# One reduction instruction for the scores of two heads in the maximum pass

## What is computed

```python
scores = jnp.einsum('bhqd,bhkd->bhqk', q, k) / jnp.sqrt(jnp.float32(dk))
scores = jnp.where(mask[:, None, None, :] == 0, neg_inf, scores)
scores = jnp.where(future[None, None, :, :], neg_inf, scores)
attn = jax.nn.softmax(scores, axis=-1)
context = jnp.einsum('bhqk,bhkd->bhqd', attn, v)
```

## Time and profile before

| | |
|---|---|
| median of 3 runs | 720.61 us (720.42 to 721.02) |
| span of the profiled execution | 718.9 us |
| TensorE busy | 653.6 us, 91% |
| VectorE busy | 516.2 us, 72% |
| ScalarE busy | 386.0 us, 54% |
| maximum pass on VectorE (L892) | 640 reductions, 333.1 us |

### The profile page before, as it was taken

One profiled execution on the slowest core, in us unless ns is written; L12 is line 12 of the kernel. 1 busy time (PEld: TensorE's weight loads), 2 busy tenths in 40 slices (PEclk: granted clock), 3 DMA queues, 4 the chain that ended last, 5 costly groups with the idle time before them and its releaser, 6 DMA issues.

```text
span 718.9 us, 11481 instructions
## 1 busy us (share of the span) xinstructions
PE 653.6 (91%) x4148; PEld 346.1 (48%) x4148; DVE 516.2 (72%) x1071; ACT 386.0 (54%) x762; POOL 68.8 (10%) x122
## 2 busy tenths in 40 slices
PE   5424989999989999999899999899998999999996
PEld 2313545546544345444333343333321388888885
DVE  4113888776897987787889788888944288777764
ACT  2210246664766675665867756567788633432331
POOL 3030440140001000220000000000000000000000
PEclk9775999999999999999999999899999999999999
DMA  9599697018001000039200130000000430607000
GB/s 297 90 136 131 109 127 78 3 36 98 2 2 19 2 1 1 2 74 160 77 1 1 45 74 1 1 1 2 1 2 1 67 52 1 133 17 140 6 31 30
DMA packets 36464, 36.87 MB, mean 51 GB/s; under 512 B 4471, under 2 KB 31447, under 8 KB 36408
## 3 DMA queue, kind: packets, MB, share of 16 engines
q1 hardware_dynamic: 33878, 33.65, 27.4%
q10 hardware_dynamic: 2530, 2.50, 1.1%
HBM read 27.94 MB, written 7.77 MB: 50 GB/s over the span
## 4 chain that ended last, share of the span: by engine, by line
PE 78%; DMA 9%; DVE 6%; ACT 3%; issue 2%; SPq 1%; POOL 1%; DVEq 0%; ACTq 0%; POOLq 0%
PE bank L1158 17%; PE ring L1118 15%; PE bank L1142 15%; PE ring L1219 4%; DMA qaug<-q_parts 4%; PE ring L1220 4%; PE ring L1221 4%; PE ring L1050 4%; PE bank L1050 4%; DVE pmax L892 3%; DMA q_parts<-stage 2%; PE bank L1236 2%; PE bank L1238 2%; PE bank L1237 2%; DMA k_parts<-stage 2%
## 5 line engine op out<-in xcount | busy, mean ns | idle before, releaser
L892 DVE TENSOR_REDUCE pmax<-ring 128x1 f32<-128x512 f32 (+4 forms) x640 | 333.1, 576 | 86.5 <-PE ring L1121 43.9
L769 ACT ACTIVATE probs<-bank 128x512 f32<-128x512 f32 (+4 forms) x592 | 286.7, 550 | 133.4 <-PE bank L1142 84.7
L1118 PE MATMUL ring<-kaug,qaug 97*128 97x512 bf16 (+4 forms) x640 | 201.9, 345 | 29.1 <-DMA qaug<-q_parts 23.3
L1142 PE MATMUL bank<-qaug,kaug 99*128 99x512 bf16 (+4 forms) x592 | 201.9, 357 | 6.4 <-ACT probs L769 5.5
L1158 PE MATMUL bank<-probs,vaug 128*32 128x512 f32 (+4 forms) x1184 | 143.2, 556 | 0.0
L1118 PEld LDWEIGHTS ring<-kaug,qaug 97*128 97x128 bf16 x640 | 61.3, 99 | 158.3 <-DVE pmax L892 82.2
L1142 PEld LDWEIGHTS bank<-qaug,kaug 99*128 99x128 bf16 (+1 forms) x592 | 57.2, 99 | 66.8 <-ACT probs L769 32.4
L796 ACT ACTIVATE u_sb<-u_sb 128x512 f32<-128x512 f32 x32 | 20.2, 632 | 59.2 <-DVE u_sb L1005 59.1
L1219 PE MATMUL ring<-x_hi,w_hi 128*128 128x512 f32 x128 | 50.4, 394 | 0.0
L1220 PE MATMUL ring<-x_lo,w_hi 128*128 128x512 f32 x128 | 50.2, 392 | 0.0
L1221 PE MATMUL ring<-x_hi,w_lo 128*128 128x512 f32 x128 | 49.8, 389 | 0.0
(11 more groups left out here) (110 smaller groups left out, 641.7 us busy)
## 6 DMA issues: line engine op xcount, KB each, us to landing
qaug<-s_dram SPq DMA_DIRECT2D x4, 2048.0 KB, 15.5
qaug<-q_parts SPq DMA_DIRECT2D x24, 256.0 KB, 9.3
kaug<-k_parts SPq DMA_DIRECT2D x18, 256.0 KB, 9.3
q_parts<-stage SPq DMA_DIRECT2D x8, 384.0 KB, 2.6
k_parts<-stage SPq DMA_DIRECT2D x6, 384.0 KB, 12.0
x_sb<-in_x ACTq DMA_DIRECT2D x4, 512.0 KB, 11.8
w_sb<-in_w SPq DMA_DIRECT2D x4, 512.0 KB, 5.4
out<-x_sb SPq DMA_DIRECT2D x4, 512.0 KB, 3.2
```

Source lines behind the costliest of these rows:

```text
L769: act.activation(probs[0:rows, u % NSLOT, h, off:CH], side_bank(e)[0:rows, off:CH], ACT.Exp, scale=DK ** -0.5).then_inc(side_read, 1)
L892: dve.tensor_reduce(pmax[:, n % 2, qt, h, slot:slot + 1], bank[:, 0:w], AX_X, ALU.max).then_inc(ring_read, 1)
L1118: last = pe.matmul(bank[:, b0:b1], qaug[0:ROW_MAX, c % 2, 4 * g + h, P * qt:P * (qt + 1)], kaug[0:ROW_MAX, 4 * g + h, k0 + b0:k0 + b1], st ...
L1142: last = pe.matmul(bank[0:r, off:CH], kaug[0:ROWS, 4 * g + h, P * j:P * j + r], qaug[0:ROWS, c % 2, 4 * g + h, off:CH], start=True, stop=n ...
```

## The change

Two heads of a group form one item. `max_pieces` yields (query tile, pair of heads, first key, width, diagonal, slot), the pair outermost; there are half as many items. Every `mx` item takes two ring banks and starts on an even one. TensorE writes the first head's scores into the first bank and the second head's into the second, each with its mask where it is on the diagonal, and signals once, after the last. VectorE reduces both with one instruction over a view of 128 partitions, 2 banks, w columns, into two neighbouring heads of `pmax`. `max_schedule` counts such an item for twice its width, so that the pace in columns is as before. Nothing else is changed.

```diff
+GP = 2
@@ max_pieces
-    for h in range(4):
+    for pr in range(GP):
...
-                out.append((qt, h, k0, w, i < KT and k0 + w == seen, slot))
+                out.append((qt, pr, k0, w, i < KT and k0 + w == seen, slot))
@@ max_schedule
-        total = sum(w / P for _, _, _, w, _, _ in pieces)
+        total = sum(2 * w / P for _, _, _, w, _, _ in pieces)
...
-            done += w / P
+            done += 2 * w / P
@@ ring_places
-        banks = 2 if e[0] == "mx" and max_pieces(e[1])[e[2]][3] > CH else 1
+        banks = 2 if e[0] == "mx" else 1
@@ ring_bank
-            return ring[:, CH * first:CH * (first + (2 if e[0] == "mx" and first % 2 == 0 else 1))]
+            return ring[:, CH * first:CH * (first + (2 if e[0] == "mx" else 1))]
@@ VectorE, mx
-                    qt, h, k0, w, _, slot = max_pieces(n)[k]
-                    dve.tensor_reduce(pmax[:, n % 2, qt, h, slot:slot + 1], bank[:, 0:w], AX_X,
+                    qt, pr, k0, w, _, slot = max_pieces(n)[k]
+                    dve.tensor_reduce(pmax[:, n % 2, qt, GP * pr:GP * (pr + 1), slot],
+                                      bank.rearrange("p (b k) -> p b k", b=2)[:, :, 0:w], AX_X,
                                       ALU.max).then_inc(ring_read, 1)
@@ TensorE, mx
-                    for b0 in range(0, w, CH):
-                        b1 = min(b0 + CH, w)
-                        cut = diagonal and b0 <= d < b1
-                        last = pe.matmul(bank[:, b0:b1], qaug[0:ROW_MAX, c % 2, 4 * g + h, P * qt:P * (qt + 1)],
-                                         kaug[0:ROW_MAX, 4 * g + h, k0 + b0:k0 + b1], start=True, stop=not cut)
-                        if cut:
-                            last = pe.matmul(bank[:, d:b1], ident_b[:, :], tri_qk[:, 0:b1 - d], start=False, stop=True)
+                    for b in range(2):
+                        h = 4 * g + GP * pr + b
+                        last = pe.matmul(bank[:, CH * b:CH * b + w], qaug[0:ROW_MAX, c % 2, h, P * qt:P * (qt + 1)],
+                                         kaug[0:ROW_MAX, h, k0:k0 + w], start=True, stop=not diagonal)
+                        if diagonal:
+                            last = pe.matmul(bank[:, CH * b + d:CH * b + w], ident_b[:, :], tri_qk[:, 0:w - d],
+                                             start=False, stop=True)
                     last.then_inc(ring_full, 1)
```

More of the change, by code:

```diff
@@ L1104, in _ @@
                     c, g = n // G, n % G
-                    qt, h, k0, w, diagonal, _ = max_pieces(n)[k]
+                    qt, pr, k0, w, diagonal, _ = max_pieces(n)[k]
                     if k == 0:
```

## The result

The changed kernel takes 751.8 us (median of 4 runs, 749.9 to 753.2) against 720.8 us of the kernel before (720.4 to 721.5), a ratio of 1.044 with a 95% interval of 1.041 to 1.047. The forecast was 751. The total is right; the experiments show that several of its terms are not, and that it is in part luck that their errors cancel.

A forecast was written before the change was run, and what follows sets the result against it. TensorE's stream of columns was taken to bound the kernel. From a median of 720.6 us, 16 + 5 + 4 + 9 + 1 - 4 = +31 gave 751.6, rounded to 751 us; range 727 to 773.

The forecast's parts named there:

- What bounds the kernel: From 105 to 530 us TensorE's column stream sets the time; VectorE's saved time gives back 4 us, ends 0 and 11.
- The price of the merge: On VectorE, each merge saves about 0.064 us, 20.5 us for 320; the rate per column holds over two banks.
- 40 us in records: Sign on VectorE: its busy time falls by some 40 us in records, overlapping tails included, while the span grows.
- The slot's round trip: In the ring, a slot holding a pair of 512 is free 1.93 us after TensorE starts the pair.
- the 65 column pairs: In chunk 3, 32 pairs each take a whole slot; stalls of 0.99 or 0.16 us, 16 us together, bounds 5 and 32.
- What makes the slot late: In the ring, TensorE starts a pair only after the pair two before is reduced, VectorE only after both matmuls.
- a bank is free at t + 1.17, with three more banks to fill meanwhile: In the kernel before, a single bank is released 1.17 us after its matmul starts (0.43 + 0.68 + 0.06).
- Before attention starts: From 63 to 105 us, VectorE idles while TensorE fills pairs, taking back the saving: +1 us, bounds -3 and +4.
- Chunks 1 and 2: Pairs of 384 and 256 stall where three fit a unit: 5 us in chunk 2, 4 in chunk 1, bounds 0 and 20.
- the single banks: Transposes taking one bank send the next pair to the slot just ahead: 5 plus 4 us, together 9, bounds 3 and 20.
- 512, 384, 512: In chunk 2, three such pairs in one unit: TensorE back after 1.48 us, slot free at 1.93, stall 0.45 us.
- rival 2: Whole kernel: stalls a third larger and the low clock after idling three more times, +50 us, 771 us; chance 0.17.

The follow-up runs named there:

- e3_two_reads: The changed kernel with each pair's merged reduction split into two of one bank each, both still started after both matmuls: 755.5 us, ratio 1.050.
- The ladder: Five kernels adding to the kernel before, one by one, neighbouring heads, due at once, even banks, TensorE's joint wait, VectorE's joint wait: 728.2, 734.9, 737.4, 746.8, 755.5 us.
- e11_adjacent: The kernel before with the two heads' pieces next to each other, each with its own bank, wait, signal, reduction and due position: 728.2 us, ratio 1.014.
- e1_order: The kernel before with the two heads' pieces next to each other and due at once, each with its own bank, wait, signal and reduction: 734.9 us, ratio 1.019.
- e5_no65_after: The changed kernel without the 65 column pieces of chunk 3: 734.6 us, ratio 1.016.
- e4_no65_before: The kernel before without the 65 column pieces of chunk 3: 716.9 us, ratio 0.994.
- The even cut: The changed kernel with chunk 3's keys cut into 401, 401, 401, 398 columns: 740.4 us, ratio 1.026; the kernel before cut likewise: 719.8 us, 0.999.
- e8_singles_before: The kernel before with 64 more single-bank items, four per group's maximum pass, each one small matmul and one small VectorE copy: 740.3 us, ratio 1.029.
- e12_joint_wait: The kernel before with twos due at once on even banks, TensorE waiting for both banks, VectorE starting on the first at once: 746.8 us, ratio 1.037.

## Why the prediction was right, and where it was not

**What bounds the kernel: right.** TensorE's stream sets the time. VectorE's 20 us came back as 3 by the medians and 6 to 7 at equal clock (e3_two_reads against the change); the forecast took 4, between 0 and 11.

**The price of the merge: right.** 64 ns each and a rate that holds over two banks, by the shapes above. The line of the forecast that VectorE's time would fall by some 40 us in records holds for the sum of the records (640 of 576 ns on average against 320 of 1008, 46 us less); the busy time of the page counts overlapping tails once and fell by 17.

**The slot's round trip: right.** 1.93 us forecast, 1.92 in the timeline; and the 65 column pairs, the largest term, at 13 us against 16.

**What makes the slot late: half right.** The forecast laid the whole growth on two banks being handed over at once. The ladder gives the joint wait and the late start 18 us (21 at equal clock); 13 to 16 us (12 to 15) come from the order of the pieces and the even banks, which it treated as costless. The step that failed is the comparison "a bank is free at t + 1.17, with three more banks to fill meanwhile": that holds for pieces one score matmul apart in the old order, and the change moves two heads' pieces together, the 65 column ones above all. The total came out because the stalls overlap: behind two 65s TensorE loses 0.39 us (491.27 - 490.82 - 0.06) when the pieces are only neighbours, and 0.99 in the change. The forecast worked out the last of these with all steps in it, and so had priced the order without naming it. The rest is luck: 3 us too few before attention stand against 3 too many for the 65 column pairs.

**Before attention starts: too small.** +1 forecast, +4.0 measured, the upper bound given. With neighbours alone the stage takes 48.2 us (63.0 to 111.2 in e11_adjacent), due at once 50.4 (63.2 to 113.6 in e1_order), in the change 49.9, before 45.9. So it is the order again that was missing. The granted clock may have a part: 0.87 against 0.91 from 63 to 105 us, and in the change from 105 to 112 us

```profile
105.00:112.00 7.00, 5.81 (x31) 2.46 (x30) 5.56 (x9) 2.96 (x4) 2.48 (x6) 0.76 0.40 117
```

which is 7 x 0.24 = 1.7 us. TensorE had idled again and again just ahead; that this is the cause is only argued. The part is small: e3_two_reads, the change without the merge, takes 49.3 us for the stage (63.2 to 112.5), 3.4 more than before, at a granted clock of 1.00 from 72 us on, as before the change.

**Chunks 1 and 2 and the single banks: order of size.** 18 us forecast together (5 + 4 + 9); without the 65s the change is 17.7 us over its control, of which 2 belong before attention (62.0 to 110.1 in e5_no65_after, 63.2 to 109.7 in e4_no65_before). The 17.7 hold what the merge gives back too, for which the forecast took 4 off, so the stalls themselves are some 3 to 7 us more than the 15.7 left. How they divide was tested for the singles alone: 0.28 us a place, so 26 places are 7 us of the 9. The even cut says that three pairs of 401 in a unit are cheaper than worked out; for the mixed pairs of chunks 1 and 2 no run tells it apart. Two details of the forecast are off. For 512, 384, 512 its own terms give 1.43 us (0.44 + 0.22 + 0.33 + 0.44) and not 1.48, 0.4 us in eight walks. And a maxima transpose takes 0.41 us of the stream (363.47 in the rows above: 0.09 + 0.32) and not 0.22, so that its stall without a value step is 0.64 us and not 0.83, some 1 us in twelve places.

**The rivals.** The fall of the clock at 463 us is gone, and two others came, the one just shown and one from 220 to 228 us, at a mean of 0.57 (8 x 0.43 = 3.4 us). Together 5 us against 3.4, so some 2 us of the 31 and not the 10 of rival 2; the times at equal clock say the same (29.2 us over the kernel before instead of 31.0). Score matmuls waiting for ScalarE did not grow.

## What to carry to other kernels

A merge of instructions on an engine that isn't the bound is worth what the bound waits for that engine, 3 to 7 of 20 us here, and it is paid in buffers when it hands over several at once: work out the round trip of a buffer, from the producer's start to the consumer's release, against the producer's shortest way back to it, at the places where a small piece or a single item breaks the regular row. Count the producer's lead in buffers, not in bytes; a small item that takes a whole buffer, or two of them side by side, halves it. Merge what fits into one buffer: it saves instructions and buffers together, here 4.5 us. And when steps of a few us are compared, look at the granted clock of the runs: corrected for it, one step of this ladder doubles and another loses a third.

## What the runs showed of the hardware

Changing the width of the weights costs TensorE time, the narrow weights do not. Matmuls with 8 columns of weights and 128 streamed follow each other every 0.056 us, but 0.09 us pass ahead of the first and 0.09 behind the last, between them and matmuls of 128 columns of weights (L1128 in the kernel before, L1130 in e8_singles_before). The same 0.09 us stand ahead of the value matmuls, with their 32 columns of weights, in every unit.

The run-to-run spread of one kernel is mostly its granted clock: 6.2 us for 0.01 of mean clock, with 0.8 us left.

One VectorE reduction over two PSUM banks (128 x 2 x 512) took 1222 ns, two of one bank 684 each with 0.60 us from one start to the next, so 1.28 us to the end of the second (e3_two_reads, e12_joint_wait).
